# Counting source nodes inside the attention-scores pass, with three encoding banks two pairs ahead

## What is computed

```python
# attention: one score for each edge and head, before the softmax over edges
alpha = jnp.einsum('ehd,hd->eh', h_src, a_src) + jnp.einsum('ehd,hd->eh', h_dst, a_dst)
enc = jax.nn.relu(edge_attr @ edge_W.T + edge_b).reshape(-1, H, D)
alpha = alpha + jnp.sum(enc * h_dst, axis=-1)
...
# graph convolution: how often each node is a source
deg = jnp.zeros((n,), input_feature.dtype).at[row].add(1.0) + 1.0
dinv = deg ** (-0.5)
norm = (dinv[row] * dinv[col])[:, None]
```

## Time and profile before

| | us |
|---|---|
| median of 3 runs (6805.44 to 6826.25) | 6811.75 |
| the profiled execution | 6786.33 |
| its span in the profile | 6784.7 |
| scores pass, from the first one-hot table to the last score | 98.3 to 964.3 |
| one iteration of it, from one burst of gathers to the next | 31.7 to 34.7 |
| degrees, from the first DMA to the last one issued | 2247.1 to 2325.7 |

### The profile page before, as it was taken

How to read it: one execution, slowest core, us unless ns; L and a number is a source line. 1 busy time by engine, 2 the same in 40 slices (tenths; PEclk the granted TensorE clock), 3 DMA queues, 4 the chain that set the end, 5 groups by cost and what they waited for, 6 DMA issues and landing times. The chain is left out here.

```text
span 6784.7 us, 97259 instructions
## 1 busy us (share of the span) xinstructions
PE 4343.0 (64%) x21805; PEld 3583.0 (53%) x21806; DVE 3048.1 (45%) x6902; ACT 1972.4 (29%) x4303; POOL 2764.5 (41%) x3021
## 2 busy tenths in 40 slices
PE   4666643652996467775776566675676757775392
PEld 3444433542885356664666555564565646664261
DVE  4433457752001645554454544455454445555303
ACT  1111110010231034442444434442444424444120
POOL 2444422533002155553555445553555535553101
PEclk8787766975998588887888788887888878887596
DMA  4555563632453144442444344343443424442131
GB/s 137 158 160 156 159 190 95 176 91 79 184 192 127 35 125 122 116 121 87 116 123 116 88 121 114 108 118 92 116 115 109 117 87 119 121 116 72 47 108 53
DMA packets 461211, 794.76 MB, mean 117 GB/s; under 512 B 221403, under 2 KB 278412, under 8 KB 450551
## 3 DMA queue, kind: packets, MB, share of 16 engines
q0 software_dynamic: 130720, 364.17, 19.4%
q1 hardware_dynamic: 322967, 401.22, 19.0%
q10 hardware_dynamic: 7488, 28.97, 1.4%
HBM read 671.50 MB, written 123.52 MB: 117 GB/s over the span
## 5 line engine op out<-in xcount | busy, mean ns | idle before, releaser
L1730 POOL DMA_INDIRECT g_g<-xl_table,g_idx x2080 | 1968.0, 946 | 1663.3 <-issue 1146.3
L1774 PE MATMUL g_b<-g_onehot,g_msg 128*128 128x128 f32 x8320 | 1375.9, 319 | 893.3 <-DVE agg L1862 336.4
L1774 PEld LDWEIGHTS g_b<-g_onehot,g_msg 128*128 128x128 f32 x8320 | 1296.6, 229 | 1109.8 <-DVE agg L1862 796.8
L1862 DVE TENSOR_TENSOR agg<-agg,g_b 128x256 f32 x2080 | 868.0, 417 | 1331.8 <-remote 854.0
L1761 PE MATMUL g_b<-g_we,g_ea 128*128 128x256 f32 x4160 | 1291.4, 441 | 185.9 <-DVE g_msg L1849 92.4
L1761 PEld LDWEIGHTS g_b<-g_we,g_ea 128*128 128x128 f32 x4160 | 844.8, 225 | 302.0 <-DVE g_msg L1849 112.9
L1833 ACT ACTIVATE g_msg<-g_msg 128x512 f32<-128x512 f32 x1040 | 650.8, 626 | 1124.5 <-DVE g_msg L1849 1002.7
L1849 DVE TENSOR_TENSOR g_msg<-g_g,g_b 128x512 f32<-128x512 f32 x1040 | 710.4, 683 | 483.4 <-remote 222.2
L544 PE MATMUL sc_pe_h<-ae_h_rows,sc_onehot 128*128 x1664 | 506.9, 456 | 218.5 <-DVE sc_prod L616 152.4
L512 POOL DMA_INDIRECT sc_g<-h_table,sc_idx x416 | 399.5, 960 | 452.9 <-DVE sc_alpha L608 330.0
L544 PEld LDWEIGHTS sc_pe_h<-ae_h_rows,sc_onehot 128*128 128x128 f32 x1664 | 348.4, 220 | 332.1 <-issue 272.7
(11 more groups left out here) (256 smaller groups left out, 3536.0 us busy)
## 6 DMA issues: line engine op xcount, KB each, us to landing
g_ea<-in_ea SPq DMA_DIRECT2D x260, 512.0 KB
ex_w<-in_f_w SPq DMA_DIRECT2D x80, 1024.0 KB, 7.4
e_rows<-sc_g SPq DMA_DIRECT2D x208, 272.0 KB
g_g<-xl_table,g_idx POOLq DMA_INDIRECT x2080
at_g<-e_rows ACTq DMA_DIRECT2D x52, 544.0 KB, 4.0
at_g<-e_rows SPq DMA_DIRECT2D x52, 544.0 KB, 3.7
xl_table<-g_rows SPq DMA_DIRECT2D x25, 640.0 KB, 4.0
sc_rel<-rel_row SPq DMA_DIRECT2D x52, 256.0 KB
```

The lines of the kernel that those rows point to most:

```text
L1730: nc.gpsimd.indirect_dma_start(out=g.g[:, j, :], out_offset=None, in_=k.xl_table[:, :], in_offset=bass.IndirectOffsetOnAxis(ap=g.idx[:, q, ...
L1774: last = nc.tensor.matmul(ps[u % (SB // 2)][:, at:at + P], g.msg[:, j, b * P:(b + 1) * P], g.onehot[:, j, :], start=True, stop=True)
L1862: nc.vector.tensor_tensor(window, window, ps[u % (SB // 2)][:, i * D:(i + 1) * D] .rearrange("p (b n) -> p b n", b=K), ALU.add).then_inc(g ...
```

## The change

The degree count moves into the scores pass. In each iteration DVE makes the two source tables right after the product of pair 2 (`hot_sources`), and PE counts right after the expansion of pair 3 (`count`), which waits for them; there is one buffer of each table. The accumulating bank `ps_deg` takes one of the eight banks, so `pe_e` keeps three (`BANK` says which pair uses which, `FREE` how many relus back the bank's last reader lies) and PE encodes two pairs ahead. SP loads the source numbers ahead of everything else in the pass, DVE splits them at its start, and at its end one instruction writes `deg`. The stage `degrees` keeps only what follows the count, and `h` and `dinv_row` are allocated and zeroed there.

```diff
-    EB, HB, RING = 4, 2, 4
+    EB, HB, RING = 3, 2, 4
+    BANK = [0, 1, 2, 0, 2, 0, 1, 2]
+    FREE = [3, 3, 3, 3, 2, 2, 3, 3]
...
+            sp.dma_start(src[:], a["src_cols"]).then_inc(src_loaded, 16)
             for q in range(2):
                 load_rows(q, rows_of(q, 0))
...
-                pe.wait_ge(relu, it * PAIRS + u + 1)
+                pe.wait_ge(relu, it * PAIRS + u + 1 + EB - FREE[u])
...
                 for u in range(PAIRS):
-                    if u + 1 < PAIRS:
-                        encode(it, u + 1)
+                    if u + 2 < PAIRS:
+                        encode(it, u + 2)
                     elif not final:
-                        encode(it + 1, 0)
+                        encode(it + 1, u + 2 - PAIRS)
                     expand(it, u, blocks)
+                    if u == 3:
+                        count(it, final)
+
+            def count(it, final):
+
+                pe.wait_ge(hot_src, it * 2 + 2)
+                for j in range(BODY):
+                    last = nc.tensor.matmul(ps_deg[0:NT, 0:P], tile_hot[:, j, :], place_hot[:, j, :],
+                                            start=False, stop=final and j == BODY - 1)
+                last.then_inc(counted, 1)
...
+            dve.wait_ge(src_loaded, 16)
+            nc.vector.tensor_scalar(hi[:], src[:], 7, None, ALU.arith_shift_right).then_inc(halved, 1)
+            nc.vector.tensor_scalar(lo[:], src[:], P - 1, None, ALU.bitwise_and).then_inc(halved, 1)
...
+            def hot_sources(it):
+
+                dve.wait_ge(counted, it + 1)
+                cols16 = bass.ds(it * BODY, BODY)
+                for of, to, width in ((hi, tile_hot, NT), (lo, place_hot, P)):
...
                     if u == 1:
                         hot_half(it, 1)
+                    if u == 2:
+                        hot_sources(it)
...
+            dve.wait_ge(counted, ITERS + 1)
+            nc.vector.tensor_scalar(k.deg[:], ps_deg[0:NT, 0:P], 1.0, None, ALU.add).then_inc(deg_out, 1)
...
 def degrees(k):
...
+    k.h = k.ctx.enter_context(nc.sbuf_tensor("h", [P, K, ACC], F32))
+    k.dinv_row = k.ctx.enter_context(nc.sbuf_tensor("dinv_row", [P, ACC], F32))
...
         @block.scalar
         def _(act):
-            act.wait_ge(added, 1)
             nc.scalar.activation(deg[:], deg[:], ACT.Sqrt).then_inc(root, 1)
```

More of the change, by code:

```diff
@@ L1508, in degrees @@
     nc, a = k.nc, k.a
+    k.h = k.ctx.enter_context(nc.sbuf_tensor("h", [P, K, ACC], F32))
+    k.dinv_row = k.ctx.enter_context(nc.sbuf_tensor("dinv_row", [P, ACC], F32))
+    deg = k.deg
     with ExitStack() as c:
         sem, sb, bank = makers(k, c, "dg")
-        src, hi, lo = (sb(n, [P, ET], I32) for n in ("src", "hi", "lo"))
-        tile_hot = sb("tile_hot", [P, 2, BODY, NT], BF16)
-        place_hot = sb("place_hot", [P, 2, BODY, P], BF16)
-        deg = sb("deg", [NT, P])
         cols = sb("cols", [P, NT, 2])
-        ps = [bank(f"ps{i}") for i in range(2)]
-        loaded, split, hot, counted, added, root, done, turned, stored = map(sem, (
-            "loaded", "split", "hot", "counted", "added", "root", "done", "turned", "stored"))
+        ps = bank("ps")
+        root, done, turned, stored, blank = map(sem, ("root", "done", "turned", "stored", "blank"))
         block = c.enter_context(nc.Block())
@@ L1522, in _ @@
         def _(sp):
-            sp.dma_start(src[:], a["src_cols"]).then_inc(loaded, 16)
             sp.wait_ge(done, 1)
@@ L1537, in _ @@
             v = nc.vector
[L1538 to L1560 removed]
+            v.memset(k.h[:, :, NP:ACC], 0.0).then_inc(blank, 1)
+            v.memset(k.dinv_row[:, NP:ACC], 0.0).then_inc(blank, 1)
             dve.wait_ge(root, 1)
@@ L1563, in _ @@
             dve.wait_ge(turned, 1)
[L1564 to L1565 removed]
+            v.tensor_copy(cols[:, :, 0], ps[:, 0:NT]).then_inc(turned, 1)
+            v.tensor_scalar(cols[:, :, 1], ps[:, 0:NT], -1.0, None, ALU.mult).then_inc(turned, 1)
+            dve.wait_ge(turned, 3)
         @block.tensor
         def _(pe):
[L1569 to L1582 removed]
             pe.wait_ge(done, 1)
[L1584 removed]
+            nc.tensor.transpose(ps[:, 0:NT], deg[:], k.ident[0:NT, 0:NT]).then_inc(turned, 1)
         @block.scalar
         def _(act):
[L1588 removed]
             nc.scalar.activation(deg[:], deg[:], ACT.Sqrt).then_inc(root, 1)
```

63 lines of the change are left out of this document (21 added, 42 removed).

## The result

The changed kernel took 6872.27 us in the median of 8 runs (6852.28 to 6895.54), the kernel before, run beside it on the same chip, 6828.18 us (6782.11 to 6837.1). The ratio is **1.0076** with a 95% interval of 1.0048 to 1.0104: slower by 44 us, or three quarters of a per cent. The forecast was 6869 us, made of +57 us and the median of 6811.75 us that the kernel before had then; the rest of this document goes by the difference, 44 us against 57.

A forecast was written before the change was run, and what follows sets the result against it. Each iteration was bound by a gather burst DVE can't get through, then a serial tail. Added tail 130 us, start and end 1.5, less 74 for the degrees: +57 on 6811.75, 6869 us; range 6735 to 6900.

The forecast's parts named there:

- the added tail: Scores pass: tables and count start pair 4's expansion 5.0 us later in each of 26 iterations, 130 us.
- the hold: Scores pass: DVE's waits for PE stay blocked while POOL gathers and end with the burst; cause not named.
- The burst, the tail and the 22.8 us: Scores pass iteration: 22.8 us of gathers, 9.3 from product 2 to the scores, 1.05 to the next burst; 33.2 us.
- G: Scores pass: start of an iteration's burst of 16 gathers; product 2 was to stay at 22.8 us after it.
- The upper end: Scores pass: 6.1 us added per iteration, 159 us, if expansions drop to the lower clock, as the skill's recurring-wait rule suggests.
- Iteration 7: Scores pass of the kernel before: the one of 25 bursts where product 2 got through early and product 3 was held.
- Work put into the burst is then free: Scores pass: work beside the gathers costs nothing, work between product 2 and the scores is paid in full.
- the first one: Scores pass: rival that the tables fall into the burst and cost nothing, about 6739 us; chance 0.20.
- The low clock through the whole tail: Scores pass: rival that TensorE stays at 1.2 GHz, expansion 5 too, 48 us more, 6917 us; chance 0.08.
- The second, POOL's: Scores pass: rival that tables delay gathers, at most 74 us, 6813 us; chance 0.12 shared with half the iterations escaping.
- The degrees: Stage of the degrees: the root on ACT no longer waits for the count, only its table load; gain 74.2 us.
- The encodings two ahead: Scores pass: PE encoding two pairs ahead costs and saves nothing; taken as 0, between -7 and +3 us.

The follow-up runs named there:

- no_count: The changed kernel with the tables and the count left out of the loop: 6772.05 us, ratio 0.9929 to the kernel before.
- late_alloc: The kernel before with only `h` and `dinv_row` allocated and zeroed in the stage of the degrees: 6803.65 us, ratio 0.9989.
- tables_in_burst: The changed kernel with tables made behind the product of pair 0 and counted behind the expansion of pair 1: 6672.96 us, ratio 0.9795 to the kernel before.
- pause_only: The kernel before with POOL waiting for DVE's product of pair 1 ahead of the gathers of pair 2: 6712.19 us, ratio 0.9825.
- no_count_one_ahead: The changed kernel without tables and count, encodings one pair ahead, still three banks: 6774.48 us, ratio 0.9925 to the kernel before.
- change_pause: The changed kernel with POOL waiting for product 1 ahead of pair 2's gathers, on a third chip: 5592.05 us, ratio 1.0042 to the kernel before there.

## Why the prediction was right, and where it was not

**The number is better than its parts.** The forecast was +57 us and +44 were measured. That 6869 and 6872.27 lie 3 us apart is luck: the median of the kernel before, run beside the changed one, was 16 us above the one that I had started from. And within the 57 two errors go against each other: the term of the added tail was too large, by 24 to 43 us, and the graph layers, which I had left out since no line of them changes, brought some 31. What was right is the way of the change and its mechanism: the tables and the count stand behind the hold, in the tail, and are paid there.

**The burst, the tail and the 22.8 us: right where the sum needs them.** Product 2 stood at G + 22.7 in 24 of 25 iterations, the tables right behind it and the count behind those. Pair 4's expansion started 5.79 us after product 2 (1053.36 to 1059.15), where I had worked out 5.8. The distance became 37.24 us, where I had 38, and POOL's wait 432 us, where I had 460. "A burst that DVE can't get through" was too strong: in 24 of the 25 bursts of before the product of pair 1 gets through in the middle of it, at G + 12.2 to G + 19.2 (215.97 in the earlier trace rows), after a long wait.

**The size of the added tail: somewhat too large.** I took 5.0 us x 26 = 130 us. Between the two profiled executions the tail grew by 13.86 - 9.27 = 4.6 us in the mean of 24 iterations, and the pass by 106 us. Against no_count it is 100 us by the ratios, and 13.86 - 10.29 = 3.6 us an iteration by the traces. Two things made my term too large. The start of pair 4's expansion was put right, but not what follows. The expansion comes right behind the count, and took 3.04 to 3.71 us there, not the 3.88 that it had behind a wait; and pair 5's took 2.05, where it was 2.4 to 2.6 in most iterations of late_alloc and no_count. I had left both as they were. And I had read the tail of 9.3 us as a constant of the kernel before, while late_alloc, with the same code in the pass, has 10.27: it moves with how many of the expansions take the time of the lower clock (in before 7.85 us where pair 4's took 2.04, 10.3 where it took 3.88). Measured from 10.3, less is added than from 7.85. The measured 87 to 106 us lie at the lower bound of the term, 101 us, and partly below it. I had made that bound from a faster count, and the count was not faster (1.89 us in all but one iteration), so where it fits it does so by luck. The upper end, 159 us, which by the rule that I had set beside it would be the nearer one, was not approached: pair 4's expansion took some 3.1 us, between the 2.04 and 3.88 of the two clock levels, and pair 5's ran at the full clock.

**Iteration 7 again.** It was the exception before, and it is one in the profile after. Here the product of pair 2 came at G + 12.65 and the tables fell into the burst:

```profile
374.91 0.57 DVE L627 TENSOR_TENSOR sc_tile_hot<-iota_row,sc_hi 128x400 bf16<-128x400 f32 x1
374.96 1.34 POOL L518 DMA_INDIRECT sc_g<-h_table,sc_idx  x1 [0.30 <-issue]
375.40 2.28 DVE L627 TENSOR_TENSOR sc_place_hot<-iota_row,sc_lo 128x2048 bf16<-128x2048 f32 x1
376.61 1.89 POOL L518 DMA_INDIRECT sc_g<-h_table,sc_idx  x1 [0.30 <-issue]
...
391.06 0.95 POOL L518 DMA_INDIRECT sc_g<-h_table,sc_idx  x1 [6.30 <-DVE sc_alpha L644]
```

Two gathers were slowed, by 1.3 us together (1.34 and 1.89 in place of 0.95), and still the next burst came after 29.4 us (361.64 to 391.06), against 32.8 in the same iteration before. That line led to tables_in_burst.

**"Work put into the burst is then free": too weak.** It was worth more than nothing. Of the 140 us that tables_in_burst gained, 74 are the degrees; the other 66 and what the graph layers took back came from the pass, 88 us in the profile, and by pause_only from the broken hold. I had written that the forecast needed only that the hold ends with the burst; that was enough for this change and would have led me wrong on the better one.

**The rivals.** The tables fell into the burst in one iteration of 25, so the first one didn't come. The low clock through the whole tail didn't either: pair 5's expansion took 2.05 us in every iteration. The second, POOL's, has a real mechanism, and on two chips a price of the wrong sign: the gather beside a table takes 1.9 to 2.9 us, but there a delay of POOL pays. On the third chip, where no hold is there to be broken, it costs some 1.8 us an iteration by the account above; I had 2.86 as the most.

**The degrees: right.** 74.2 us gone in the profile, as worked out.

**The encodings two ahead: right at 0**, by no_count against no_count_one_ahead. **The two allocations: no cost seen** in late_alloc (-27 to +13 us by its interval). **The rest, "which has no edit in it": not 0**, but some 31 us in the graph layers of every kernel built on the changed one. **Start of the pass**: the first product at 105.84 in place of 105.01, +0.8, where I had +1.5.

**What stays open.** What in the change lengthens the graph layers was not found: each of those traces is one execution, and late_alloc, which has only the two allocations moved, has 3927.8 us there and belongs to the other group. And what it is in the chip that holds DVE's and ACT's waits for PE while POOL issues gathers was not found; the runs only say what it goes with (gathers in a row, at both widths tried), what relieves it (2 to 3 us without one) and that one chip of three doesn't have it.

## What to carry to other kernels

Find the stretch of the loop in which the engine isn't the bound, and put added work there; the same count costs 100 us behind the hold and comes with a gain inside the burst, two pairs earlier in the same loop. Add up the stages that you didn't touch as well, over several kernels: here one without an edit took 31 us more. Where a wait ends at a fixed distance from another engine's burst, whatever the waited-for work does, try a pause in the burst: it is one line, and here it was worth nearly as much (1.75%) as the best place for the count (2.05%). But measure such a gain on more than one chip: on the third one the changed kernel with the pause was 0.4% slower than the kernel before, and no part of the gain was seen.

## What the runs showed of the hardware

- On two of three chips, while POOL issues indirect gathers back to back (one per 1.25 us), DVE and ACT see PE's finished matmuls late: from about 5 us after the burst's start to about 3 us after its end, 16.2 us in the longest wait shown here. One wait is let through in between (the product of pair 1, G + 12.2 to 19.2 in before). Narrow rows don't change it (G + 22.85 with 8 numbers a row).
- The issue of DMAs on SP is slow in the same stretch. SP's timeline of before, and then that of change_pause on the third chip, where it isn't:

```profile
203.81 0.02 SPq L443 DMA_DIRECT2D sc_idx<-in_src_halves  x1
207.37 0.01 SPq L446 DMA_DIRECT2D sc_rel<-rel_row  x1
208.82 0.01 SPq L449 DMA_DIRECT2D sc_ea<-ea_parts  x1
```

```profile
199.61 0.61 SPq L448 DMA_DIRECT2D sc_idx<-in_src_halves  x1
200.47 0.51 SPq L451 DMA_DIRECT2D sc_rel<-rel_row  x1
201.16 0.32 SPq L454 DMA_DIRECT2D sc_ea<-ea_parts  x1
```

  From the first of three issues to the last it is 5.0 us in the one and 1.6 in the other. Over the whole pass it is at most 1.9 us in change_pause, and over 2 us in 26 of 52 cases in before.
- Three chips differ by 18% on the same program (5567 us, and 6820 to 6837), while single instructions take the same: 0.95 us a gather, 0.70 a product.
- A gather that starts while DVE makes a table from two SBUF tiles ends 0.82 us after the table: 1.89 to 2.86 us in place of 0.95 beside the large table (26 of 27 gathers of tables_in_burst), 1.34 beside the small one in iteration 7 of the changed kernel.
- Two executions of the same code in the pass (before and late_alloc, which differ in two addresses) had tails of 9.27 and of 10.27 us in the mean, 20 us over the pass.
